# The order of counting-step reads and squares on ScalarE in two graph-attention passes

## The reference, cut to what matters

```python
# layer 1, run twice (4 heads, then 1 head)
e = leaky_relu(a_src[src] + a_dst[dst], 0.2)
p = exp(e - segment_max(e, dst)[dst])
alpha = p / (segment_sum(p, dst) + 1e-16)
out = segment_sum(h[src] * alpha, dst)
# layer 2, run three times
agg = segment_sum(h[edge_src], edge_dst)
h = relu(h @ Ws + (agg * inv_deg) @ Wn + b)
```

## Time and profile before

| what | value |
|---|---|
| median of 3 runs | 3394.49 us (3393.63 to 3402.31) |
| the profiled execution | 3403.45 us, of which the span is 3401.5 us |
| busy: PE, DVE, ACT, POOL | 74%, 64%, 49%, 46% of the span |
| first pass with counting steps | 745 to 1362 us |
| second pass with counting steps | 1413 to 1940 us |
| PE's granted clock over the span | 0.787 |

### The profile page before, as it was taken

One profiled execution on the slowest core, in us unless ns is written; L12 is line 12 of the kernel. 1 busy time (PEld: TensorE's weight loads), 2 busy tenths in 40 slices (PEclk: granted clock), 3 DMA queues, 4 the chain that ended last, 5 costly groups with the idle time before them and its releaser, 6 DMA issues.

```text
span 3401.5 us, 48599 instructions
## 1 busy us (share of the span) xinstructions
PE 2525.2 (74%) x11507; PEld 1942.9 (57%) x11507; DVE 2164.6 (64%) x5185; ACT 1652.9 (49%) x3627; POOL 1567.4 (46%) x1656
## 2 busy tenths in 40 slices
PE   6777777757777777457777766989988994777765
PEld 4665665434555455235455555778777874666653
DVE  5888887456666665556656666434555556666668
ACT  2887887515455454345555534432222444444443
POOL 4777771077777730377777700000000005777770
PEclk9999999856566666555666558999999997888887
DMA  6555552035554431344444415776777864555550
GB/s 207 156 160 156 159 161 66 25 84 110 109 112 109 108 86 43 78 103 109 105 112 108 104 61 175 264 244 208 249 254 258 282 240 148 158 154 156 158 153 22
DMA packets 391112, 489.16 MB, mean 144 GB/s; under 512 B 168377, under 2 KB 265710, under 8 KB 385888
## 3 DMA queue, kind: packets, MB, share of 16 engines
q1 hardware_dynamic: 324934, 288.34, 28.2%
q0 software_dynamic: 63088, 192.63, 20.9%
q10 hardware_dynamic: 2828, 5.18, 0.5%
HBM read 384.00 MB, written 101.90 MB: 143 GB/s over the span
## 4 chain that ended last, share of the span: by engine, by line
PE 40%; DVE 20%; POOL 13%; issue 11%; DMA 9%; ACT 3%; DVEq 2%; SPq 1%; ACTq 0%; POOLq 0%
POOL y_and_h L731 11%; PE ps L986 10%; DMA rows<-in_ea_swept 8%; PE ps L1071 7%; PE ps L863 5%; PE ps L1002 4%; PE ps L998 3%; DVE y_and_h L1701 3%; DVE big L1673 3%; PE ps L950 3%; DVE ps L1693 2%; POOL big L717 2%; DVE ps L2182 2%; PE ps L799 1%; PE ps L785 1%
## 5 line engine op out<-in xcount | busy, mean ns | idle before, releaser
L717 POOL DMA_INDIRECT big<-table_gat,src_idx x832 | 801.0, 963 | 634.4 <-DMA table_gat<-y_and_h 317.6
L1673 DVE TENSOR_TENSOR big<-big,ps 128x257 f32 (+3 forms) x1664 | 593.6, 357 | 303.2 <-PE ps L986 81.5
L1430 ACT ACTIVATE w_sb<-ps 128x200 uint16 x784 | 262.0, 334 | 577.5 <-PE ps L1002 573.6
L731 POOL DMA_INDIRECT y_and_h<-table_pool,src_block x391 | 375.6, 961 | 178.1 <-issue 118.9
L702 POOL DMA_INDIRECT big<-table_mlp,src_block x391 | 370.9, 949 | 157.7 <-issue 116.1
L1477 ACT ACTIVATE big<-big 128x3432 f32<-128x3432 uint16 (+1 forms) x72 | 210.1, 2919 | 479.4 <-PE ps L1071 479.4
L746 POOL DMA_DIRECT2D big<-adj x36 | 19.2, 532 | 781.8 <-ACT big L1477 704.3
L998 PE MATMUL ps<-extra 128*128 128x200 bf16 x784 | 263.1, 336 | 56.8 <-issue 28.0
L863 PE MATMUL ps<-w_sb,ea_sb 128*128 128x256 f32 x832 | 210.4, 397 | 127.2 <-DVE y_and_h L1701 116.7
L1071 PE MATMUL ps<-big,y_and_h 128*128 128x264 f32 (+1 forms) x1200 | 293.7, 394 | 0.0
L1229 PE MATMUL ps<-big,y_and_h 128*128 x624 | 194.7, 466 | 115.2 <-DVE big L2288 113.9
(11 more groups left out here) (349 smaller groups left out, 5364.6 us busy)
## 6 DMA issues: line engine op xcount, KB each, us to landing
big<-adj POOLq DMA_DIRECT2D x33, 1650.0 KB, 8.2
rows<-in_ea_swept SPq DMA_DIRECT2D x194, 256.0 KB, 3.3
adj<-w_sb SPq DMA_DIRECT2D x784, 50.0 KB
ea_sb<-in_ea_blocks SPq DMA_DIRECT2D x416, 64.0 KB
ea_sb<-rel_rows SPq DMA_DIRECT2D x208, 128.0 KB
prefix_blocks<-rows SPq DMA_DIRECT2D x97, 256.0 KB, 2.2
rows<-prefix_blocks SPq DMA_DIRECT2D x97, 256.0 KB, 3.1
below_blocks<-ea_sb SPq DMA_DIRECT2D x97, 256.0 KB, 2.6
```

The costliest lines, as they stand in the source:

```text
L717: pool.indirect_dma_start(ring[:, step % GAT_RING, :], None, table[k], bass.IndirectOffsetOnAxis(src_idx[:, step:step + 1], 0))\
L731: pool.indirect_dma_start(pool_rows[q][:, i, :], None, table["pool"], bass.IndirectOffsetOnAxis(src_block[:, block:block + 1], 0)).then_in ...
L1430: act.activation(staging[:, (4 * quad + j) % STAGED, :], ps[:, 6:8, :][:, bass.ds(halves_of[j + 1], 1), 0:CW].rearrange("p o n -> p (o n)" ...
L1673: dve.tensor_tensor(to, to, bank_of(j), ALU.add).then_inc(accumulated, 1)
```

## The change

In `square_steps_of` the call of `between(j)`, which in the attention passes is `read_step(j)`, now stands ahead of square j and not behind it. The same instructions run. In passes without `between` (the fourth) nothing moves, nor do slots without a quad change their order.

```diff
--- before.py
+++ after.py
@@ -1378,12 +1378,12 @@
                 if g >= n:
                     act.wait_ge(summed, base[k] + g - n + 1)
                 for j in range(G):
+                    if between:
+                        between(j)
                     ins = act.activation(onehot_of(k, g)[:, j, :], iota[:, 0:P], ACT.Square,
                                          bias=dst_rel[:, g * G + j:g * G + j + 1], scale=-1.0)
                     if j == G - 1:
                         ins.then_inc(squares_ready, 1)
-                    if between:
-                        between(j)
 
             def mark_nodes_of(k, g, between=None):
```

## The result

The changed kernel took 3426.1 us (median of 4 runs, 3419.5 to 3429.2) beside 3396.6 for the kernel before in its runs up to then. The ratio of the two is 1.0067, 95% interval 1.0046 to 1.0088: slower, by some 23 us, while the medians themselves are 29.5 apart. The profiled execution took 3419.46 us, of which its span is 3417.6. That span is only 16 us longer than the one of before: what stands behind the start of the last read, which the change does not touch, took 1453 us in it and 1462 in the kernel before, and between 1453 and 1476 in the ten executions that have a trace. So I read the change's cost in a trace from the stretches that it touches.

What follows compares the result with a forecast made beforehand. A PE-DVE chain bounds each batch, with ACT setting the first read at borders with marks. 1.52 us a batch over 21 batches, 31.9, plus 1.5 for last slots: 33.4 on 3394.5, so 3428 us; range 3404 to 3448.

Steps and rivals of the forecast that it cites:

- The Relu's wait: At the border, the Relu waits for the square directly ahead, starting 0.42 us behind it; alone 0.13 us more border.
- The register load: At the border, the 0.55 us load starts with the waiting Relu and no longer lies hidden under it.
- Rival (a): At the border, the load stays hidden, leaving only the Relu's wait: 0.35 us a batch, 3402.5 us; chance 0.13.
- The tail behind the load: At the border, from the load's end to the next read, with one more wait to pass: 0.25 us.
- The slack: At count 1, PE has `add_terms` to do, so the first 0.09 us of a first read's delay is free.
- Count 1: PE's count behind a slot's first read: 0.24 us later, from a border 0.33 us longer less 0.09 of slack.
- place 0: Slot where the stage DVE waits for stands behind count 1, so the stall moves along: 0.24 us paid.
- Place 7: Slot where PE stalls behind count 1 for DVE's `add_terms`; the delay goes into the stall: 0 us.
- The first 16 slots of the second pass: They wait for the gathers of two batches anyway, so they pay nothing; slots 16 to 89 pay.
- The sum: Over both passes: 1.52 us a batch times 21 batches, 31.9 us; with the first pass's last slots 33.4 us.
- A changed pattern of grants: Sign of being wrong in the profile after: PE's clock granted in other slots, which would point to rivals (b, c).
- rival (c): Longer borders get PE's clock granted in more slots, making it faster; all 63 lower-level slots would give 3381; chance 0.03.

Runs made afterwards that it cites:

- the kernel with the last square early: The change, but with the last square ahead of the last read, so the Relu follows a read; 0.9990 of the kernel before, 3 us less.
- the one with the last pair turned: Kernel before with only read 3 put ahead of square 3, squares 0 to 2 still ahead of their reads; 60 us slower (55 to 65).
- the two single-pass totals: The change in the first attention pass alone and in the second alone, against the kernel before: 14 and 15 us slower.

## Why the prediction was right, and where its sizes were off

**What bounds it.** The border between slots, where ACT goes through Relu and a square without a pause, sets when count 1 can go. That was right: the kernel with the last square early takes ACT out of the border, and the one with the last pair turned puts more in, and the time follows, from a border of 1.05 us (-3 us, not clear of none) over 1.14 (before), 1.29 (+5) and 1.43 (+22) to 1.58 (+60).

**The Relu's wait.** Forecast 0.42 behind the square, seen 0.43.

**The register load.** Forecast: it starts with the waiting Relu. It does (1004.9 for 1004.85 above). The Trainium skill's page Perfetto Trace Analysis, in its part on DVE and ACT instructions, would have the sequencer go on as soon as the waiting operation is in the wait queue; this trace does not agree for a register load, which began with the waiting Relu and 0.43 us behind the start of the square ahead of it. Rival (a), a hidden load, would have cost 8 us; with the load really out of the way it was 5. The tail behind the load was forecast at 0.25 and is 0.22, so the border is 1.43 and not 1.47.

**The slack and the places.** Count 1 is 0.20 later and not 0.24, since the border is shorter. At place 0 it is 0.12: last to second read was 2.34 there before, and with it the slack 0.2 and not the 0.09 that I read at one other place and used for all. Place 7 takes the delay into its stall: its slots went from 7.13 to 7.10 in the first pass. Place 3, behind which DVE waits, paid in full (6.93 to 7.21). The first 16 slots of the second pass paid nothing, as forecast: they took 87.8 us before and after.

**The sum.** This is the term that was off: I had 31.9 us for the 168 slots, and the two executions of the change show 21.0 and 22.6. About 6.7 us of the difference is the border and the slack as above (0.04 less at four places and at place 2, 0.12 at place 0, times 21). Most of the rest goes with PE's clock. Slots of the first pass in one batch of the kernel after, places 4, 5, 6 and 7 (columns as in the earlier trace rows):

```profile
1004.19:1009.27 5.08, 4.54 (x20) 3.16 (x20) 2.99 (x10) 3.24 (x9) 3.86 (x5) 0.55 0.56 126
1009.27:1013.93 4.66, 3.95 (x21) 2.54 (x21) 2.98 (x10) 3.23 (x9) 3.44 (x5) 0.81 0.56 131
1013.93:1018.97 5.04, 4.54 (x20) 3.15 (x20) 2.92 (x9) 3.23 (x9) 1.71 (x3) 0.50 0.60 132
1018.97:1026.10 7.13, 4.64 (x20) 3.14 (x20) 4.19 (x12) 3.23 (x9) 5.61 (x6) 0.74 0.34 77
```

In the batch of before that is read in the earlier trace rows, place 6 had 0.88 of the clock and took 4.11; now it has 0.50 and takes 5.04, while place 5 has 0.81 and takes 4.66. In the means of the first pass place 6 is 0.57 us longer and place 5 is 0.30 shorter, though count 1 is late by 0.2 at both. Slots that were mostly at the upper level number 12 of 12 at place 6 and 1 of 12 at place 5 before, 7 and 11 after. A changed pattern of grants stood among the prediction's own signs of being wrong; it came about, beside the forecast mechanism and not in its place. Over the stretch more of the clock is granted. Slots 10 to 103 of pass 1 and 16 to 89 of pass 2, first before:

```profile
748.07:1304.65 556.58, 408.11 (x1930) 287.01 (x1930) 350.82 (x1099) 289.05 (x871) 346.56 (x362) 0.60 0.46 103
1500.51:1939.38 438.87, 322.20 (x1528) 223.04 (x1528) 271.09 (x886) 226.12 (x684) 314.09 (x329) 0.60 0.47 108
```

and after:

```profile
750.74:1318.66 567.92, 414.72 (x1929) 280.77 (x1929) 351.45 (x1098) 308.61 (x870) 348.34 (x362) 0.63 0.44 101
1516.15:1964.65 448.50, 330.57 (x1527) 222.56 (x1527) 271.11 (x886) 242.16 (x685) 320.46 (x335) 0.61 0.46 106
```

The mean clock went from 0.60 to 0.63 in the first pass, and to 0.62 and 0.63 in the other two kernels with this border there, while the other kernels have 0.60 or 0.61. From the trace of the clock, PE was at its upper level, 2.4 GHz, for 116 us of the first stretch before and for 143 after, and for 92 and 102 of the second. A straight line through the 36 plain slots of the first pass before, each one's length against its time at the upper level, falls by 0.18 us for a microsecond at that level. So these 38 us give back an estimated 7. By that 31.9 less 6.7 less 7 is 18, beside the 21.0 and 22.6 seen; 3 to 4 us stay open, with one trace of the kernel before to compare with. That is rival (c) at a small size, on top of the forecast. In the first pass it is clear of the scatter: the three traces with this border there have 140 to 147 us at the upper level, the seven others 113 to 123. In the second pass it is not: its three traces have 96 to 102 us, the others 55 to 99. Why a PE that waits more was granted more is not shown by any run here; in the kernel with the last pair turned, where PE waits longer still, it was granted about as much as before (120 us for 116).

**Luck.** The median of 3426.1 lies 2 us from the forecast of 3428, and that is closer than the reasoning earned: I forecast 33 us of loss, and the two ratios give 22 to 23. The absolute number came out because the kernel before ran at a median of 3396.6 rather than 3394.5 in the comparison, and because the medians of the two kernels lay 29.5 us apart, more than the ratio gives. The batches became 1.0 us longer, not 1.5.

**Still open.** The order of the grants by slot (place 5 for place 6) and its link to the length of a batch; the last 3 to 4 us of the sum; what the kernel with the last pair turned loses beyond its delays; the two single-pass totals, which sum to more than the whole, though within their intervals.

## What to carry to other kernels

In a loop that is written out by hand, look at the border between turns and not only at the order inside one: swapping two operations in the body changed nothing there, but put a square directly ahead of the operation that waits for it. An operation of the same engine whose result is waited for wants another operation between. A register load behind an instruction that waits starts only with that instruction, so it wants either another place (0.15 us of border came back) or an operation behind it that hides it, as the square did in the kernel with the last pair turned. Ask too for how long the other engine would not have noticed: here the first 0.1 us of a delay was free at most places and 0.2 at one, and a stall for a third engine swallowed nearly all of it at one place in eight. And hold the clock fixed when slots are compared: the mean of places 4 to 6 mixes the delay with grants that moved.

## What the runs showed of the hardware

A register load of 0.54 us on ACT began with the activation ahead of it that waited, 0.005 us behind its start in the median, and the next read followed the load's end by 0.22. It cost nothing where it began 0.19 us ahead of the 128x512 Relu, and 0.15 us a border where it began with it and a read stood next. An ACT operation that waits for the one directly ahead of it starts 0.42 to 0.43 us behind it, where an independent square starts 0.29 behind. And with a border 0.3 us longer PE's clock was at its upper level in other slots and for longer, 143 of 567.9 us of the first pass's stretch in place of 116 of 556.6, which by estimate returned some 5 us there. A plain slot with no time at that level took 4.82 us; the slots of before with more than 3.3 us of it took 4.11.
